# A fused attention, binary convolution, depthwise and linear attention kernel: one root and a fold moved in their queues, the depthwise taps reordered, fillers and a new order in the tail

## Time and profile before

| what | value |
| --- | --- |
| three timed runs, median | 76.19 us (76.15 to 77.23) |
| the profiled execution, its own time | 75.42 us |
| its span, from the first to the last instruction | 73.7 us |
| mean granted TensorE clock over the span | 0.977 |
| busy: TensorE, VectorE, ScalarE, GpSimd | 62.6, 44.6, 30.7, 31.3 us |

### The profile page before, as it was taken

The page is one execution under the profiler, slowest core; times in us unless marked ns, Lnnn a source line. Parts: engine busy times, 40 slices in busy tenths (PEclk is TensorE's granted clock), DMA queues, the critical chain, the costliest instruction groups (busy, mean ns, idle before and its releaser), DMA issues.

```text
span 73.7 us, 1931 instructions
## 1 busy us (share of the span) xinstructions
PE 62.6 (85%) x704; PEld 49.0 (67%) x704; DVE 44.6 (60%) x167; ACT 30.7 (42%) x89; POOL 31.3 (42%) x92
## 2 busy tenths in 40 slices
PE   3979999999992999958998899999554999999900
PEld 2645888888991984517886578875142988999600
DVE  3779654467554997888366970065697447635630
ACT  5102031848990510029008780060383848784200
POOL 6706858988895312530002007006448519620000
PEclk9999999999999999999999999999998579999999
DMA  0897210000000000000000000000000000000124
GB/s 2 201 387 160 38 21 0 0 0 0 0 13 0 4 0 0 0 0 9 0 0 0 0 0 9 9 0 9 4 0 0 0 0 0 0 0 0 63 88 147
DMA packets 2778, 2.14 MB, mean 29 GB/s; under 512 B 976, under 2 KB 2512, under 8 KB 2768
## 3 DMA queue, kind: packets, MB, share of 16 engines
q1 hardware_dynamic: 2768, 2.01, 9.5%
HBM read 1.49 MB, written 0.52 MB: 27 GB/s over the span
## 4 chain that ended last, share of the span: by engine, by line
PE 43%; POOL 28%; DVE 13%; issue 9%; ACT 2%; POOLq 0%; ACTq 0%; DVEq 0%
PE bank L1455 7%; PE bank L1394 6%; POOL conv_blocks L394 4%; POOL gn_rstd L363 4%; PE bank L1540 3%; PE bank L1521 3%; PE bank L1531 3%; POOL x_bias L382 3%; PE bank L1586 3%; PE bank L1381 3%; PE bank L1566 2%; PE bank L1296 2%; PE bank L1410 2%; DVE h_linear L1092 2%; POOL bn_rstd L363 2%
## 5 line engine op out<-in xcount | busy, mean ns | idle before, releaser
L363 POOL TENSOR_TENSOR gn_rstd<-gn_var_eps,minus_half 128x1 f32<-128x1 f32 (+2 forms) x12 | 7.4, 620 | 8.3 <-DVE gn_var_eps L812 8.0
L1280 PE MATMUL bank<-warm 128*128 128x256 bf16 x36 | 7.0, 357 | 1.1 <-POOL warm L347 1.1
L1455 PE MATMUL bank<-x,dw_diag 32*32 32x256 f32 x288 | 7.6, 381 | 0.3 <-DVE x L1055 0.3
L1455 PEld LDWEIGHTS bank<-x,dw_diag 32*32 32x32 f32 x288 | 5.2, 103 | 1.6 <-issue 0.9
L1280 PEld LDWEIGHTS bank<-warm 128*128 128x128 bf16 x36 | 4.5, 129 | 2.4 <-POOL warm L347 1.1
L664 ACT ACTIVATE h<-bank,l_shift,dw_scale 128x256 f32<-128x256 f32 x4 | 2.2, 560 | 7.4 <-PE bank L1483 7.1
L1394 PE MATMUL bank<-signs,conv_blocks 128*128 128x256 bf16 x36 | 4.3, 276 | 1.2 <-ACT signs L602 1.2
L1357 PE MATMUL bank<-k,q 128*128 128x256 f32 x16 | 5.0, 444 | 0.0
L602 ACT ACTIVATE signs<-res,bn_shift,bn_scale 128x256 bf16<-128x256 f32 x4 | 2.2, 595 | 6.6 <-DVE bn_shift L996 6.6
L1394 PEld LDWEIGHTS bank<-signs,conv_blocks 128*128 128x128 bf16 x36 | 3.4, 97 | 2.2 <-issue 1.6
L1092 DVE TENSOR_SCALAR_CACHE_REDUCE h_linear<-bank,dw_scale 128x256 f32<-128x256 f32 x4 | 1.9, 480 | 4.6 <-PE bank L1483 4.6
(11 more groups left out here) (186 smaller groups left out, 160.5 us busy)
## 6 DMA issues: line engine op xcount, KB each, us to landing
out<-x SPq DMA_DIRECT2D x4, 128.0 KB, 2.4
late_params<-in_late SPq DMA_DIRECT2D x1, 404.5 KB, 4.9
x<-in_x SPq DMA_DIRECT2D x1, 384.0 KB, 3.6
early_params<-in_early SPq DMA_DIRECT2D x1, 258.0 KB, 3.8
x<-in_x SPq DMA_DIRECT2D x1, 128.0 KB, 2.1
pw_weights<-in_late SPq DMA_DIRECT2D x2, 64.0 KB, 3.8
pw_weights<-in_late SPq DMA_DIRECT2D x4, 32.0 KB, 1.8
l_params<-in_late SPq DMA_DIRECT2D x4, 2.2 KB, 1.7
```

Source lines behind the costliest of these rows:

```text
L363: return nc.gpsimd.tensor_tensor(out_ap, in_ap, minus_half[:, 0:n], ALU.pow)
L1280: nc.tensor.matmul(bank[:, 0:N], warm[:, 0:C], warm[:, :], start=True, stop=True)
L1455: nc.tensor.matmul(tile_of(p, i, r), dw_diag[of, tap, :], xs[2][of, 2 * p + i, dy:dy + H, dx:dx + W], start=(tap == 0), stop=False)
```

## The change

- GpSimd: `dw_diagonals` is gone; `sw_root` stands directly behind `x_bias(3)`; `group_swaps` moves between the two batch-norm roots; `gn2_scale(0)` goes ahead of `gn2_mean_diag(0)`; `norm_bias_out` is made for image 1 alone; `rinv3_out(0)` and `(1)` move up.
- ScalarE: nine `dw_diagonal(tap)` around `q_out(0)` and `setup_out`; `norm3_first(0)` is gone; the tail has another order, `q3_out(3)` among it.
- VectorE: `tile_consts` moves behind `gn_mean_sq(0, 0)`; `means2(1)` one call up; `norm3(0)` new; the tail in another order.
- TensorE: each tap of `valid_taps` waits for its own diagonal; all nine taps of pair 0 and `less_mean(0)` run ahead of pair 1's taps; fillers of 5, 4 and 4 matmuls stand around `group_means3(0)` and `(1)`, ahead of `pointwise(1)`; the tail in another order, with `output(0)` ahead of `project_v3(3)`.

```diff
--- before.py
+++ after.py
@@ -206,6 +206,7 @@
         pw_ps = [banks[i][:, 0:N] for i in (6, 2, 3, 4)]
         linear_ps = [banks[3][:, 0:N], banks[4][:, 0:N]]
         late_warm_ps = banks[6]
+        gap_warm_ps = banks[5]
         l2_row_ps = banks[4][:, N:N + C]
         k3_ps = [banks[(6, 2)[b % 2]][:, 0:N] for b in range(B)]
         vt_ps = banks[5][:, 0:N]
@@ -433,15 +434,6 @@
                                                   ALU.mult, ALU.add)
                 ins.then_inc(group_swap_ready, 1)
 
-            def dw_diagonals():
-
-                pool.wait_ge(late_in, 16)
-                pool.wait_ge(ident_tile_ready, 1)
-                nc.gpsimd.tensor_tensor(
-                    dw_diag[:, :, :], ident_tile[:, :].unsqueeze(1).to_broadcast([C, TAPS, TILE]),
-                    lp[:, LC["dw"]].unsqueeze(2).to_broadcast([C, TAPS, TILE]),
-                    ALU.mult).then_inc(dw_diag_ready, 1)
-
             def head_masks():
                 step(nc.gpsimd.memset(head_mask[:, :], 1.0))
                 same_block(head_mask, HEAD).then_inc(head_mask_ready, 1)
@@ -513,19 +505,18 @@
             x_bias(1)
             x_bias(2)
             x_bias(3)
-            dw_diagonals()
+            sw_root()
             l2_constants()
-            group_swaps()
             conv_weights()
-            sw_root()
             gn_root(1, 0)
             gn_root(1, 1)
             gn_root(1, 2)
             gn_root(1, 3)
             bn_root(0)
+            group_swaps()
             bn_root(1)
+            gn2_scale(0)
             gn2_mean_diag(0)
-            gn2_scale(0)
             gn2_scale(1)
             gn2_mean_diag(1)
             out_bias_less_floor(0)
@@ -534,20 +525,19 @@
             x3_sum_less_floor(1)
             mean_with_floor(0)
             gn_root(3, 0)
-            norm_bias_out(0)
             mean_with_floor(1)
+            gn_root(3, 1)
+            norm_bias_out(1)
             out_bias_less_floor(2)
-            gn_root(3, 1)
             x3_sum_less_floor(2)
-            norm_bias_out(1)
             out_bias_less_floor(3)
             x3_sum_less_floor(3)
+            rinv3_out(0)
             mean_with_floor(2)
             gn_root(3, 2)
             mean_with_floor(3)
+            rinv3_out(1)
             gn_root(3, 3)
-            rinv3_out(0)
-            rinv3_out(1)
             rinv3_out(2)
             rinv3_out(3)
         @block.scalar
@@ -565,6 +555,14 @@
                 nc.scalar.activation(setup[:, :, :].rearrange("p a c -> p (a c)"), setup_ps[:, 0:2 * C],
                                      ACT.Copy).then_inc(setup_done, 1)
 
+            def dw_diagonal(tap):
+
+                if tap == 0:
+                    act.wait_ge(ident_tile_ready, 1)
+                at = LC["dw"].start + tap
+                nc.scalar.activation(dw_diag[:, tap, :], ident_tile[:, :], ACT.Copy,
+                                     scale=lp[:, at:at + 1]).then_inc(dw_diag_ready, 1)
+
             def valid_taps_out():
                 act.wait_ge(valid_mm, 1)
                 nc.scalar.activation(valid_sum[:, :], valid_ps, ACT.Copy, scale=-1.0).then_inc(valid_ready, 1)
@@ -644,7 +642,7 @@
 
             def norm3_first(b):
 
-                act.wait_ge(norm_bias_ready, b + 1)
+                act.wait_ge(norm_bias_ready, b)
                 nc.scalar.activation(t3[:, b, :], xs[3][:, b, :], ACT.Identity,
                                      bias=norm_bias[:, b:b + 1],
                                      scale=rstd[:, 3, b:b + 1]).then_inc(t3_ready[b], 1)
@@ -692,8 +690,17 @@
                                      scale=rinv3[:, b:b + 1]).then_inc(pj_ready, 1)
 
             act.wait_ge(setup_done, 1)
+            dw_diagonal(0)
+            dw_diagonal(1)
+            dw_diagonal(2)
+            dw_diagonal(3)
             q_out(0)
+            dw_diagonal(4)
+            dw_diagonal(5)
+            dw_diagonal(6)
             setup_out()
+            dw_diagonal(7)
+            dw_diagonal(8)
             v_out(0)
             q_out(1)
             softmax(0)
@@ -728,31 +735,31 @@
             square_sum2(3)
             relu1(0, 0)
             relu1(0, 1)
+            square_sum3(0)
+            square_sum3(1)
             relu1(1, 0)
-            square_sum3(0)
             relu1(1, 1)
-            square_sum3(1)
-            norm3_first(0)
+            norm3_first(1)
+            v3_out(0)
+            q3_out(0)
             square_sum3(2)
-            norm3_first(1)
+            softmax3(0)
             square_sum3(3)
-            q3_out(0)
-            v3_out(0)
-            softmax3(0)
+            kt3_out(0)
+            softmax3(1)
+            v3_out(1)
             q3_out(1)
-            softmax3(1)
-            kt3_out(0)
-            v3_out(1)
+            kt3_out(1)
+            project_out(0)
             softmax3(2)
-            kt3_out(1)
             v3_out(2)
+            kt3_out(2)
             softmax3(3)
-            kt3_out(2)
-            project_out(0)
             v3_out(3)
             kt3_out(3)
             project_out(1)
             project_out(2)
+            q3_out(3)
             project_out(3)
         @block.vector
         def _(dve):
@@ -823,11 +830,11 @@
                                             t_ready[layer] if layer < 3 else t3_ready[b], 1)
 
 
-            tile_consts()
             dve.wait_ge(x_in[0], 16)
             gn_stats(0, 0)
             gn_aggr(0, 0)
             gn_mean_sq(0, 0)
+            tile_consts()
             dve.wait_ge(x_in[1], 16)
             gn_stats(0, 1)
             dve.wait_ge(pool_consts, 1)
@@ -1230,45 +1237,45 @@
             prune1_max(0, 1)
             prune1_weights(0, 1)
             prune1_max(0, 0)
+            means2(1)
             prune1_weights(0, 0)
-            means2(1)
             prune2_max(0)
             prune2_floor(0)
             prune2_max(1)
             x3_out(0)
+            prune2_floor(1)
+            x3_out(1)
             prune1_max(1, 1)
-            prune2_floor(1)
+            group_out(3, 0)
             prune1_weights(1, 1)
+            group_var(3, 0)
             prune1_max(1, 0)
-            x3_out(1)
+            group_out(3, 1)
             prune1_weights(1, 0)
-            group_out(3, 0)
-            group_var(3, 0)
+            group_var(3, 1)
+            norm3(0)
             prune2_max(2)
-            group_out(3, 1)
             prune2_floor(2)
-            group_var(3, 1)
+            prune2_max(3)
             x3_out(2)
-            prune2_max(3)
             prune2_floor(3)
+            k3_max(0)
             x3_out(3)
-            k3_max(0)
+            k3_max(1)
             group_out(3, 2)
             group_var(3, 2)
-            k3_max(1)
             group_out(3, 3)
             group_var(3, 3)
             norm3(2)
+            context_out(0)
+            k3_max(2)
             norm3(3)
-            k3_max(2)
+            context_out(1)
+            k3_max(3)
+            x4_out(0)
+            context_out(2)
             q3_out(2)
-            k3_max(3)
-            context_out(0)
-            context_out(1)
-            context_out(2)
-            q3_out(3)
             context_out(3)
-            x4_out(0)
             x4_out(1)
             x4_out(2)
             x4_out(3)
@@ -1403,7 +1410,7 @@
                 if tap == 0:
                     pe.wait_ge(sum_masks, 1)
                     pe.wait_ge(exp_ready, 2 * 3)
-                    pe.wait_ge(dw_diag_ready, 1)
+                pe.wait_ge(dw_diag_ready, tap + 1)
                 dy, dx = tap // 3, tap % 3
                 for r in range(TILES):
                     of = slice(r * TILE, (r + 1) * TILE)
@@ -1444,7 +1451,7 @@
 
                 if tap == 0:
                     if p == 0:
-                        pe.wait_ge(dw_diag_ready, 1)
+                        pe.wait_ge(dw_diag_ready, TAPS)
                     else:
                         pe.wait_ge(conv_neg_ready, 2)
                     pe.wait_ge(x2_ready, 2 * p + 2)
@@ -1648,55 +1655,58 @@
             depthwise(0, 0)
             depthwise(0, 1)
             depthwise(0, 2)
-            group_means2(0)
             depthwise(0, 3)
             depthwise(0, 4)
+            group_means2(0)
+            depthwise(0, 5)
+            depthwise(0, 6)
+            depthwise(0, 7)
+            depthwise(0, 8)
+            less_mean(0)
             depthwise(1, 0)
-            depthwise(0, 5)
+            group_means2(1)
             depthwise(1, 1)
-            depthwise(0, 6)
             depthwise(1, 2)
-            depthwise(0, 7)
+            pointwise(0)
             depthwise(1, 3)
-            depthwise(0, 8)
             depthwise(1, 4)
-            less_mean(0)
             depthwise(1, 5)
             depthwise(1, 6)
-            group_means2(1)
-            pointwise(0)
             depthwise(1, 7)
             depthwise(1, 8)
             less_mean(1)
+            keep_warm(5, gap_warm_ps)
             group_means3(0)
```

(40 more changed lines are left out.)

## The result

The changed kernel takes 71.77 us as a median of four runs (71.27 to 72.79), against 76.17 (76.01 to 77.23) before: a ratio of 0.941, with a 95% interval from 0.934 to 0.947. The forecast was 73.9 with a range of 72.6 to 75.5, so it had the sign and half the size. The executions of these kernels scatter: the kernel before, run 47 more times beside the experiments, gave 73.66 to 77.95, with a mean clock of 0.908 to 0.997. Its 28 executions with a mean clock of 0.955 or less have a median of 77.35, the other 19 one of 75.36. A ratio with its interval compares only executions within 1.5% of their kernel's fastest (of the kernel before that can be two of seventeen, at 73.66 and 74.72) while a median is of all, so the two can differ, and ratios of different experiments can't be set against each other.

A forecast was written before the change was run, and what follows sets the result against it. TensorE (43%) and GpSimd (28%) were taken to bound the chain, with a wait for the root near 23 us and a TensorE-bound tail partly at half clock. -1.35 - 0.15 - 0.75 = -2.25: 73.2 profiled, 73.9 median; range 72.6 to 75.5.

The forecast's parts named there:

- part 3: Start: tile_consts (the fold) behind gn_mean_sq(0,0) lets the work behind it start 0.2 earlier: -0.15 us, bounds 0 and -0.3.
- part 1: Near 23 us: sw_root ahead of l2_constants and conv_weights removes VectorE's and TensorE's wait: -1.35 us, bounds 0 and -1.4.
- part 5: Tail: the clock should hold, but late x3_out adds waits: -0.75 us, bounds -1.2 and +0.75.
- Part 2: ScalarE: nine dw_diagonal, at most 0.40 us each, fit into idle times; costed at nothing, bounds 0 and +0.4.
- Part 4: Depthwise: unmixed taps cost TensorE +1.3 us; pair 0 gains nothing, less_mean(1) comes 1.3 later.
- rival (b): Tail: the clock falls all the same and 1.5 us comes back: -0.75, 75.4 us; 15%.
- (a): Tail: it is packed and gains its full 1.2 us: -2.7, 73.5 us; 15%.
- (c): Wait at 23 us: half replaced by VectorE, 0.7 of the 1.35 us lost: 74.6 us; 10%.
- (d): Depthwise: the clock falls where a single pair uses 8 of 16 tiles, costing 3.4 us: 77.3 us; 5%.
- (e): Tail: pair 1 sets the end and its +1.6 us passes through whole: +0.1, 76.3 us; 8%.

The follow-up runs named there:

- run 47: Not a label but a count: the kernel before, unchanged, was run 47 more times beside the experiments: 73.66 to 77.95 us.
- two fold experiments: tile_consts ahead of gn_stats(0,0) again in the changed kernel: 72.01 us, ratio 0.961; tile_consts behind gn_mean_sq(0,0) alone in the kernel before: 75.44 us, ratio 1.008.
- the mixed kernel: The changed kernel with the old, mixed order of the taps, less_mean(0) and pointwise(0), rest of the tail new: 71.72 us, ratio 0.949.

## Why the prediction was half right

The result is 2.1 us under the forecast. Of that, 1.40 lies between the profiled executions: part 3 has 0.67, the end behind the last y 0.64, part 1 0.15, and part 5 takes 0.04 back. The rest is the distance of 0.77 from the profile to the median, which came out as nothing. The largest single miss is thus the last one, and the two mechanisms that the sum had wrong are the clock of the start and the store.

**Part 1, size right, cause half right.** The wait was worth 1.50 against my 1.35, as group_means(1,0) could even overlap attend(1). But I wrote that the root's move removes it, and it is only one of two ways to remove it: with the root back in its old place the wait is 0.2. The diagonals' move to ScalarE and that of group_swaps shortened what stands ahead of the root, and the earlier x_bias moved the queue forward. I had entered the diagonals as a cost with nothing on the other side. The move is thus insurance. Alone in the old kernel it brought -1.30 at group_means(1,0) but -0.87 at the first tap, since I took VectorE's one-column operations at their undisturbed length.

**Part 2 right.** Four diagonals took 0.94 (7.23 to 8.17 in the timeline), and nothing on ScalarE was late for them.

```profile
7.23 0.94 ACT L563 ACTIVATE dw_diag<-ident_tile,late_params 128x32 f32<-128x32 f32 x4
```

That is well under my bound of 0.40 each. An estimate by the Trainium skill ("ScalarE: Activation LUTs", What ACT_TABLE_LOAD costs) is 306 ns for one and 213 for each further one, 0.94 for four; the trace agrees.

**Part 3, the first step that failed.** I wrote "-0.15; bounds 0 and -0.3" and took TensorE's rate in the start as given. The 0.22 of the fold's own path is there (the second group mean at 7.32 for 7.54). On top, the clock rose earlier: in every profile with the fold behind gn_mean_sq(0,0), which closes the idle time of 0.46 us ahead of group_means(0,0) on TensorE, the first full clock came 5.6 us or more before that of any with the fold first. The end of attend(1) moved by -0.82 in all, and by -0.86 with the fold alone in the kernel before. I had read the low rate and used it, but not asked what set it. The median times of the two fold experiments are too scattered to show this gain.

**Part 4 right**, to 0.1: less_mean(0) came 5.27 behind the first tap where I had 5.25, waiting for the diagonal (0.34, where I had 0.5), and less_mean(1) 11.45 for 11.5. Unmixed, six taps of pair 1 span 2.82 and two 1.09, so 0.43 a tap. That mixing gives 0.31 is confirmed by less_mean(1) at 10.27 in the mixed kernel; its 1.2 us became 0.57 at the last y.

**Part 5, size right, reason wrong.** -0.71 for -0.75. The dip went. TensorE entered the projections 15.0 behind the first tap where I had 15.35, and from there to the last y it took 12.45 where I had 12.1: two misses of 0.35 that cancel, which is luck. And the fillers aren't what this clock needs: with the unmixed taps the tail has no dip without them, and they cost 0.25 here. My rival (b) was judged by the fillers too.

**Left out: the store, the second step that failed.** I wrote "The last output's own sequence is as long as before" and put it at nothing. VectorE's part of it is: x4_out(3) ends 0.52 behind the last y in both. But SyncE was still issuing an earlier store: in the profile of before the second one's issue took 1.66, and the last started 1.33 behind the last y; in the changed kernel it started 0.71 behind. Landing took 1.84 and 1.83 from there. That is 0.62 of the 0.64. Whether the early first store brought it stays open, since issues of 1.85 us occur in both orders.

**The median, the third.** I carried 0.77 from the profiled execution to the median unchanged. The profile of before was one of its better executions. Others have a mean clock of 0.93 and take 77.1 to 77.95 us, as if it had been low three times as long (0.068 of 75 us is 5.1 us of full rate lost, against 0.023 of 73.7, 1.7). In the changed kernel 71.77 is both the profiled time and the median, and its four executions have 0.968 to 1.0. So none of these four is such a case, and that makes 0.75 more at the median. Which stretch was low in those executions isn't shown, since none of them was profiled; the profile with GpSimd's old front queue has one right behind the wait of 1.9 us, at 24.9 to 28.3, and that with the fold alone has 6.8 us in the tail.

Of the rivals, (a), the packed tail, gave the time nearest to the result, but for a reason that isn't what happened; (c), (d) and (e) did not occur.

## What to carry to other kernels

Before you credit a wait's end to the moved instruction, sum the queue ahead of it: three edits each shortened it here, and one of them was booked as a cost. When TensorE runs a stretch at its lower rate, ask what stands ahead of it, short idle times too; in the profiles 0.8 of the 3.65 us came with a fold that moved and closed 0.46 us of idle at 4.3 us. And take more than one profile of the kernel before: a wait can hide what another engine does, and one execution's distance from the median isn't a constant that carries over.

## What the runs showed of the hardware

- In 17 of 17 profiles the place of one VectorE operation went with TensorE's first 1.00: at 4.2 to 6.6 us with the fold behind gn_mean_sq(0,0) and no idle on TensorE at 4.3 us (12 profiles), at 12.2 to 13.7 with the fold first and 0.46 us of idle there (5 profiles).
- One-column operations of VectorE with two inputs from SBUF took longer while GpSimd ran its bf16 products: 0.43 instead of 0.15 us (TENSOR_TENSOR), 0.48 instead of 0.22 (SCALAR_TENSOR_TENSOR). Their neighbours at the same time, `sw` with 0.20 and BATCH_NORM_AGGREGATE with 0.18, took what they take elsewhere. The Trainium skill ("GPSIMD Engine Reference", Specifications) names two SBUF inputs as a case of contention between the two; the trace agrees.
- The issue of a 128 KB store on SyncE took 0.33 to 1.86 us in the 17 profiles and held up the next store's issue, without anything in the kernel that tells the long ones apart. The last store landed 1.4 us after the end of its issue in 15 of them.
